# Last stage's pieces moved into the tile steps, with PSUM packed, on one core of Trainium2

## The chip, the cores and the metric

The kernel runs on one core of one Trainium2 chip. The metric is the device time of one execution in microseconds (us). Everything is FP32, apart from one projection whose operands are split into a high and a low FP32R part. Half a per cent, about 1.4 us, is near the limit of what can be measured.

## The reference

One block of a network over x of shape (8, 512, 128): a state-space mixer and then a small gated network, each with layer norms around it and a residual. Cut to what matters:

```
x  = x + layernorm(mixer(layernorm(x)))
x  = x + layernorm(ffn(layernorm(x)))

mixer: proj = x @ W_in ; z, x_raw, B, C, dt, lam, theta = split(proj)
       B, C normalised and rotated by cumulated angles; x_raw = silu(x_raw)
       y = within-chunk products (C.B masked by decay) @ x  +  C @ state of the chunks before
       y = rms(y * silu(z)) ;  out = y @ W_out
ffn:   xk, xr = mixes of x and of x one token earlier
       r = sigmoid(xr @ W_r) ; k = relu(xk @ W_k)^2 ; out = r * (k @ W_v)
```

## The kernel before

**Tiling.** A chunk is 64 tokens. A tile holds one chunk of two batches, 128 partitions in all. There are 8 chunks (`NC_`) and 4 pairs of batches (`NQ`), so 32 tiles (`NT`); tile n belongs to chunk n // 4, and a chunk of all eight batches is four tiles. The state of a pair runs from tile n to tile n + 4.

**Stages.** First, all of x is loaded, its statistics and transposes are made, and the tables of decays, step sizes and angles are computed for all tiles (to about 43 us). Second, the tiles, software-pipelined. Third, the last stage: the residual, the layer norm and the gated network for the eight chunks, also pipelined (`chunk(k, par)` on each engine, driven by `chunks`, line 292).

**The order of the tiles.** It is written out by hand. Each engine has a function `step`, and runs its steps in order; semaphores tie the engines together.

- TensorE, `step(n)`, line 970: `project_x(n+1)`, `turn(n+1)` (transposes of B and C), `project_bc(n+2)`, `y_turn(n-1)` (transposes of y), `mix(n)` (from the state, within the chunk, new state), `score(n+1)`, `y_out(n-1)` (output projection, line 967). `mix` of tile n waits for the state sum of the tiles before it (`p_added`, n), for the mask of its own tile and for both weighted products of x.
- VectorE, `step(n)`, line 1302: `state(n-1)` (sum of new and old state, line 1223), `summed_y(n-1)` (line 1231), `mask(n)` (line 1216), some pieces of the last stage when n is 28 or more, the first weighted product of x for n + 1 (line 1209), `biased(n+2)` (line 1192), the second product, `rotations(n+2)` (lines 1197 and 1202).
- ScalarE, `step(n)`, line 654: `late_o(n-2)` (evacuates the projection's output and sums its squares), `x_gate(n+1)` (SiLU of x, line 616), `turned(n+1)`, `copy_in(n+3)`, `late_yt(n-1)`, `state_part(n)`, `squares(n+2)` (line 605, waits for `biased`), `z_gate(n+2)`, `late_ysq(n-1)`.
- GpSimd, `step(n)`, line 441: `lower_part(n+3)`, `early(n+2)` (a power, line 400, waits for the squares), `gated(n)` (y, line 439, waits for `summed_y(n)`), `token_factors(n+2)` (weights of x, line 408), `decayed_z(n+2)`, `state(n)` (line 423), and behind that, for n from 28 to 30, `factors` (a power over the columns of two chunks, line 431).

So GpSimd's step n runs beside VectorE's step n + 1, as it needs the y summed there.

**The last stage** for a chunk: `factor_terms` (VectorE), `factors` (GpSimd, power), residual (VectorE with `residual` for chunks 0 and 1, GpSimd lines 488 and 492 for the others), `stats2` and `moments2` (VectorE), the power `rstd2` (GpSimd), `norm_bias` (VectorE), `normed` (ScalarE), transposes (TensorE, line 1007), `curT` and `prevT` (ScalarE copies; the first column of each batch in `prevT` by GpSimd's `carry`), k (lines 1022, 1025), r (lines 1028, 1030), ReLU and square (ScalarE), v (line 1013), tanh (ScalarE), gating and statistics (VectorE, lines 1400 and 1404), moments, a power (line 508), the last residual (line 1388), outputs (line 720) and two stores on SP. For chunk 0 the first steps are already written into tiles 28 to 32.

**PSUM.** Eight banks of 512 columns: 0 holds z, B and C, 1 holds x, 2 the turned B and C and the state part, 3 and 4 the scores, 5 the new state, 6 turned y and the output projection, 7 y. The last stage reuses 0 (transposes), 1 (k), 2 (r) and 3 (v) once the tiles are done.

`tiles(False)` is the branch that the inputs take; `tiles(True)` (`general`) is for larger decays.

Of the kernel before, what the change touches and what calls it, by code (L numbers as in the profile page):

```python
# [22 lines left out]
F32 = mybir.dt.float32  # L23
# [7 lines left out]
L = 64  # L31
# [19 lines left out]
FAC_POW = 3  # L51
# [34 lines left out]
def build(nc, x, w_in, a_log, dt_bias, bc_bias, w_out, w_r, w_k, w_v, mu, consts, out, force_general=False):  # L86
    ctx = ExitStack()
    with ctx:
# [68 lines left out]
        scores = ctx.enter_context(nc.psum_tensor("scores", [128, R, 512], F32))  # L157
        bank += [scores[:, r, :] for r in range(R)] + [ps(n) for n in range(5, 8)]
# [20 lines left out]
        TURN_BANKS, SCALAR_BANKS, W_BANKS = (0, 1, 4, 5), (2, 3, 7), (6, 0)  # L179
        s2 = sem("tables_scalar")  # L180
# [41 lines left out]
        def flat(buf):  # L222
# [51 lines left out]
        curT = sb("curT", 128, 2, B, L)  # L274
# [9 lines left out]
        cnames = ("scaled_o x1_first x1 stats mom pow norm_bias pow3 norm_bias3 normed tr_ps tr_sb carried shifted k_ps k_relu k_act r_ps th v_ps "  # L284
                  "f stats3 res outv").split()
# [6 lines left out]
        def chunks(eng, body):  # L292


            for k in range(2):
                body(k, k % 2)
            with eng.Fori(1, NC_ // 2 - 1) as cc:
                for par in range(2):
                    body(cc * 2 + par, par)
            for k in range(NC_ - 2, NC_ + 2):  # L300
                body(k, k % 2)

        def has(k, back=0):

            return not isinstance(k, int) or 0 <= k - back < NC_

        def norms(k):

            return slice(0 if has(k, -1) else NQ, 2 * NQ if has(k, 2) else NQ)
# [42 lines left out]
        def _(pool):  # L352
# [7 lines left out]
            nc.gpsimd.memset(curT[:, 1], 0.0).then_inc(S["st_zero"], 1)  # L360
# [67 lines left out]
            def factors(c):  # L428

                cols = slice(c * 2 * NQ, (c + 1) * 2 * NQ)  # L430
                nc.gpsimd.tensor_tensor(tokc[:, 7, cols], tokc[:, 6, cols], halfn[:, 0:2 * NQ],
                                        ALU.pow).then_inc(fac_p, 1)

# [7 lines left out]
            def step(n, q, general):  # L441
# [4 lines left out]
                if isinstance(n, int) and n == NT - 1:  # L446
                    pool.wait_ge(C["mom"], MOM)
                    rstd2(0)
# [7 lines left out]
                if isinstance(n, int) and 0 <= n - (NT - NQ) < NC_ // 2 - 1:  # L456
                    pool.wait_ge(fac_v, FAC_POW)
                    factors(n - (NT - NQ))

            def rstd2(k):  # L460

                wait_past(pool, C["normed"], k * NQ)
                nc.gpsimd.tensor_tensor(frs[:, 0:NQ], fmo[:, 5, 0:NQ], halfn[:, 0:NQ], ALU.pow).then_inc(C["pow"], 1)

            def tiles(general):
                for n in range(-2, NQ):
                    step(n, n % NQ, general)
                pool.wait_ge(S["weights"], 4)
                with pool.Fori(1, NC_ - 1) as c:
                    for q in range(NQ):  # L470
                        step(c * NQ + q, q, general)
                for n in range(NT - NQ, NT):
                    step(n, n % NQ, general)
# [10 lines left out]
            def residual(c):  # L484

                rows = bass.ds(c * NQ, NQ)
                pool.wait_ge(fac_p, c // 2 + 1 if isinstance(c, int) else NC_ // 2)
                nc.gpsimd.tensor_tensor(o_all[:, rows], o_all[:, rows],
                                        tokc[:, 7, rows].unsqueeze(2).broadcast_to([128, NQ, D]), ALU.mult)\
                    .then_inc(C["scaled_o"], 1)  # L490
                pool.wait_ge(C["scaled_o"], c - 1)
                nc.gpsimd.tensor_tensor(x_all[:, rows], o_all[:, rows], x_all[:, rows], ALU.add).then_inc(C["x1"], 1)

            def carry(k, par):

                wait_past(pool, C["r_ps"], k)
                nc.gpsimd.tensor_tensor(prevT[:, :, 0:1], curT[:, 1 - par, :, L - 1:L],
                                        one[:].unsqueeze(1).broadcast_to([128, B, 1]), ALU.mult).then_inc(C["carried"], 1)

            carry(0, 0)  # L500

            def chunk(k, par):
                if has(k, -2):
                    residual(k + 2)
                pool.wait_ge(C["mom"], (k + 2) * MOM)
                if has(k, 2):
                    wait_past(pool, C["res"], (k - 2) * NQ)
                    nc.gpsimd.tensor_tensor(frs[:, NQ:], fmo[:, 5, NQ:], halfn[:, 0:NQ], ALU.pow).then_inc(C["pow3"], 1)  # L508
                if has(k, -1):
                    rstd2(k + 1)  # L510
                if has(k) and not (isinstance(k, int) and k == 0):
                    carry(k, par)
                if isinstance(k, int) and k == 1:
                    pool.wait_ge(fac_v, 2 * FAC_POW)
                    factors(NC_ // 2 - 1)

            chunks(pool, chunk)

        @block.scalar
        def _(act):  # L520

            act.wait_ge(s_a, 16)
# [131 lines left out]
            def step(n, q):  # L654
# [8 lines left out]
                if within(n - 1):  # L663
                    late_yt(n - 1)
# [772 lines left out]
```

## Time and profile before

| what | value |
| --- | --- |
| median of 3 runs | 272.7 us (271.68 to 273.03) |
| profiled execution | 273.49 us |
| its span in the profile | 271.7 us |
| busy: TensorE, VectorE, ScalarE, GpSimd | 229.7, 196.6, 194.1, 168.1 us |
| mean granted clock of TensorE | 0.963 |
| tables until about | 43 us |
| first and last output projection of a tile | 57.0 and 207.25 us |

The profiled execution took 273.49 us and its records span 271.7 us, so 1.8 us lie around the span. Busy times of TensorE count every matmul from start to modelled end; they overlap, so a sum of durations is more than the time in which they ran, and the distance between starts is the better measure. A row of the timeline gives the start (us from the span's start), the time until the last of the group ended, the engine (PE is TensorE, PEld its weight loads, DVE is VectorE, ACT is ScalarE, POOL is GpSimd), the line, the operation, the tiles written and read, and in brackets how long the engine had been idle before and whose work ended that.

### The profile page before, as it was taken

The page shows a single profiled execution, that of the slowest core. Times are in us where ns is not written, and L with a number is a line of the kernel's source. Part 1 is how long each engine was busy: PE and PEld are TensorE (multiplying, and loading weights), DVE is VectorE, ACT ScalarE, POOL GpSimd, SP SyncE. Part 2 cuts the span into 40 slices and gives each one's busy share as a digit, 9 for nine tenths or more (in the row PEclk, how much of TensorE's full clock was granted, in tenths as well). Part 3 has the DMA queues.
Part 4 walks back from the last instruction along what each step waited for, and adds up shares of the span by engine and source line. Part 5 has one row for each costly group of instructions (what it writes and reads, how often), then busy time and mean ns, then how long its engine had stood idle before and what let it go on. Part 6 is the DMA issues. An engine that isn't in the chain of part 4 may idle for free.

```text
span 271.7 us, 7118 instructions
## 1 busy us (share of the span) xinstructions
PE 229.7 (85%) x1958; PEld 176.3 (65%) x1958; DVE 196.6 (72%) x593; ACT 194.1 (71%) x727; POOL 168.1 (62%) x281
## 2 busy tenths in 40 slices
PE   0995997789899999999999999999873798989930
PEld 0993343578678788787887878877652485657730
DVE  1699999967677676776767757679565758887761
ACT  2367387689787877878778788788554386979941
POOL 6423407586686867777687786877596476774120
PEclk9999599999999999999999999999999599999995
DMA  5960000000000000000000000000000000311122
GB/s 131 224 219 2 0 0 1 0 4 2 2 2 0 2 2 0 2 0 2 2 0 0 2 2 0 2 0 4 2 0 6 5 2 1 77 36 43 41 58 58
DMA packets 10159, 6.39 MB, mean 24 GB/s; under 512 B 832, under 2 KB 9824, under 8 KB 10128
## 3 DMA queue, kind: packets, MB, share of 16 engines
q1 hardware_dynamic: 9984, 5.77, 8.5%
q8 instruction: 18, 0.29, 0.5%
q0 software_dynamic: 144, 0.21, 0.4%
q14 instruction: 13, 0.11, 0.1%
HBM read 3.88 MB, written 2.10 MB: 22 GB/s over the span
## 4 chain that ended last, share of the span: by engine, by line
PE 45%; DVE 19%; issue 14%; ACT 10%; POOL 7%; DMA 2%; ACTq 1%; DVEq 1%; POOLq 1%
PE bank L886 10%; PE bank L790 6%; PE bank L967 6%; PE bank L874 6%; PE bank L880 5%; ACT bt L627 3%; DVE f L1388 3%; POOL frs L508 3%; ACT bank L616 2%; DVE ff L1400 2%; PE bank L757 2%; DVE fst L1404 2%; DMA w_sb<-w_in 2%; PE bank L749 1%; POOL rb L400 1%
## 5 line engine op out<-in xcount | busy, mean ns | idle before, releaser
L1209 DVE TENSOR_TENSOR x<-bank,wx 128x512 f32<-128x512 f32 x32 | 22.1, 690 | 35.5 <-ACT bank L616 31.3
L886 PE MATMUL bank<-x,sg 64*64 64x256 f32 x256 | 34.6, 385 | 0.0
L886 PE MATMUL bank<-xg,sg 64*64 64x256 f32 x256 | 33.9, 376 | 0.0
L874 PE MATMUL bank<-x,turned_bc 64*64 64x256 f32 x224 | 29.6, 376 | 0.0
L439 POOL TENSOR_TENSOR y<-ysum,zs 128x256 f32<-128x256 f32 x32 | 23.7, 740 | 7.7 <-DVE ysum L1231 7.2
L397 POOL TENSOR_TENSOR mse<-msb,eps_all 128x2 f32<-128x2 f32 x32 | 6.9, 217 | 33.1 <-ACT junk L607 33.1
L880 PE MATMUL bank<-st,bt 64*64 64x256 f32 x128 | 20.8, 395 | 5.0 <-ACT bt L627 4.9
L886 PEld LDWEIGHTS bank<-xg,sg 64*64 64x64 f32 x256 | 21.5, 133 | 4.7
L400 POOL TENSOR_TENSOR rb<-mse,halfn 128x2 f32<-128x2 f32 x32 | 23.0, 717 | 2.5
L616 ACT ACTIVATE bank<-bank,rsn 128x512 f32<-128x512 f32 x32 | 21.2, 661 | 4.3 <-PE bank L790 1.4
L967 PE MATMUL bank<-wo_sb,yt 128*128 128x128 f32 x128 | 22.8, 301 | 0.5 <-ACT yt L633 0.5
L1209 DVE TENSOR_TENSOR xg<-bank,wx 128x512 f32<-128x512 f32 x32 | 21.7, 680 | 0.0
L652 ACT ACTIVATE zt<-bank 128x256 f32<-128x256 f32 x32 | 12.3, 384 | 11.1 <-PE bank L880 11.1
L865 PE MATMUL scores<-bt 64*64 64x64 f32 x256 | 20.2, 230 | 0.0
L415 POOL TENSOR_TENSOR zs<-zs,ec_all 128x256 f32<-128x256 f32 x32 | 20.2, 631 | 0.0
L508 POOL TENSOR_TENSOR frs<-fmo,halfn 128x4 f32<-128x4 f32 x8 | 8.1, 1012 | 19.2 <-DVE fmo L325 19.2
L790 PE MATMUL bank<-w_hi,x_hi 128*128 128x512 f32 x32 | 15.3, 478 | 5.5 <-DVE w_lo L1093 2.7
L874 PEld LDWEIGHTS bank<-x,turned_bc 64*64 64x64 f32 x224 | 18.0, 133 | 1.4
L886 PEld LDWEIGHTS bank<-x,sg 64*64 64x64 f32 x256 | 17.9, 132 | 1.3
L967 PEld LDWEIGHTS bank<-wo_sb,yt 128*128 128x128 f32 x128 | 16.7, 190 | 3.1 <-ACT yt L633 0.7
L865 PEld LDWEIGHTS scores<-bt 64*64 64x64 f32 x256 | 16.7, 132 | 2.3 <-ACT bt L627 0.3
L423 POOL TENSOR_TENSOR st<-sp,f_all 128x256 f32<-128x256 f32 x28 | 17.6, 629 | 0.0
(201 smaller groups left out, 771.9 us busy)
## 6 DMA issues: line engine op xcount, KB each, us to landing
x_all<-x SPq DMA_DIRECT2D x16, 128.0 KB, 3.8
out<-o_all SPq DMA_DIRECT2D x16, 128.0 KB, 2.4
cm<-consts SPq DMA_DIRECT2D x1, 640.0 KB, 6.5
w_sb<-w_in SPq DMA_DIRECT2D x1, 480.0 KB, 4.4
cm<-consts POOLq DMA_DIRECT2D x1, 128.0 KB, 3.9
wo_sb<-w_out SPq DMA_DIRECT2D x1, 128.0 KB, 4.8
bcb_sb<-bc_bias SPq DMA_DIRECT2D x1, 96.0 KB, 4.7
wr_sb<-w_r SPq DMA_DIRECT2D x1, 64.0 KB, 4.6
```

The lines of the kernel that those rows point to most:

```text
L400: nc.gpsimd.tensor_tensor(rb[:, par], mse[:], halfn[:, 0:R], ALU.pow).then_inc(S["rb_ready"], 1)
L415: nc.gpsimd.tensor_tensor(zs[:, q].rearrange("p (h e) -> p h e", e=P), zs[:, q].rearrange("p (h e) -> p h e", e=P), at(ec_all, n).unsqueez ...
L423: nc.gpsimd.tensor_tensor(st[:, q].rearrange("p (h e) -> p h e", e=P), sp[:].rearrange("p (h e) -> p h e", e=P), at(f_all, i).unsqueeze(2) ...
L439: nc.gpsimd.tensor_tensor(y[:, par], ysum[:, par], zs[:, q], ALU.mult).then_inc(S["y_ready"], 1)
L616: nc.scalar.activation(bank[1][:], bank[1][:], ACT.Silu, scale=rsn[:, par:par + 1]).then_inc(S["x_silu"], 1)
L790: mm = nc.tensor.matmul(bank[1][:], a[:, par], b[:, O_X:O_S], start=(k == 0), stop=(k == 2))
L865: mm = nc.tensor.matmul(scores[half(h), r, 0:L], bt[half(r), par, r, half(h)], bt[half(r), par, 1 - r, half(h)], start=True, stop=True)
L874: mm = nc.tensor.matmul(bank[5][half(1 - h), 0:DI], turned_bc[half(h), q, 2 * r], rx(x, r)[half(h)], start=(r == 0), stop=(r == R - 1))
L880: mm = nc.tensor.matmul(to[half(h)], bt[half(1 - h), par, h, half(h)], state[half(1 - h)], start=True, stop=True)
L886: mm = nc.tensor.matmul(bank[7][half(h), 0:DI], sg[half(h), a, r], rx(x, r)[half(h)], start=start, stop=stop)
L967: mm = nc.tensor.matmul(bank[6][:, DI:DI + D], yt[:, k], wo_sb[:, k], start=(k == 0), stop=(k == 1))
L1209: vec.tensor_tensor((x1, xg)[a][:, par].rearrange("p (a e) -> p a e", e=P), bank[1][:].rearrange("p (a e) -> p a e", e=P), wx[:, par, a].u ...
```

## The change

The last stage is cut into pieces, one chunk at a time, and each piece is put into a step of the tiles, for all chunks. Each engine gets `ffn(n)`, with `c, q = divmod(n, 4)`; it goes on for 16 steps after the tiles (`FFN_STEPS`). The loops of VectorE, ScalarE and GpSimd over chunks are written out.

```
+FFN_STEPS = NT + 4 * NQ
 # TensorE, between project_bc(n + 2) and y_turn(n - 1)
+                ffn(n - 1)
+            def ffn(n):
+                c, q = divmod(n, NQ)
+                if q == 0 and valid(c - 3):
+                    project_v(c - 3)
+                if q == 1 and valid(c - 2):
+                    turn_normed(c - 2)
+                if q == 2 and valid(c - 2):
+                    project_k(c - 2)
+                if q == 3 and valid(c - 2):
+                    project_r(c - 2)
 # VectorE, between mask(n) and the first weighted product
+                ffn(n)
+            def ffn(n):
+                c, q = divmod(n, NQ)
+                if q == 0 and valid(c - 2):
+                    norm_bias(c - 2)
+                if q == 0 and valid(c - 4):
+                    last_residual(c - 4)
+                if q == 1 and valid(c - 3):
+                    gated_v(c - 3)
+                if q == 2 and valid(c - 1):
+                    factor_terms(c - 1)
+                if q == 2 and valid(c - 3):
+                    moments3(c - 3)
+                if q == 3 and valid(c - 1):
+                    residual(c - 1)
+                    stats2(c - 1)
+                    moments2(c - 1)
 # GpSimd, at the end of the step
+                ffn(n)
+            def ffn(n):
+                c, q = divmod(n, NQ)
+                if q == 1 and valid(c - 2):
+                    carry(c - 2)
+                if q == 2 and valid(c - 1):
+                    factors(c - 1)
+                if q == 2 and valid(c - 3):
+                    rstd3(c - 3)
+                if q == 3 and valid(c - 1):
+                    rstd2(c - 1)
 # ScalarE, between copy_in(n + 3) and late_yt(n - 1)
+            def empty_ffn_bank(n):
+                c, q = divmod(n, NQ)
+                if q == 0 and valid(c - 3):
+                    gate_r(c - 3)
+                if q == 2 and valid(c - 2):
+                    turned_x(c - 2)
+                if q == 3 and valid(c - 2):
+                    k_relu(c - 2)
 # ScalarE, at the end of the step
+            def ffn(n):
+                c, q = divmod(n, NQ)
+                if q == 0 and valid(c - 2):
+                    normed(c - 2)
+                if q == 1 and valid(c - 4):
+                    outputs(c - 4)
+                if q == 3 and valid(c - 2):
+                    k_square(c - 2)
```

The residual is done by VectorE for all chunks, and `factors` takes the four columns of one chunk:

```
             def factors(c):
+                pool.wait_ge(fac_v, FAC_STEPS * (c + 1))
+                nc.gpsimd.tensor_tensor(tokc[:, 7, tiles_in(c)], tokc[:, 6, tiles_in(c)], halfn[:, 0:NQ],
...
+            def residual(c):
+                dve.wait_ge(fac_p, c + 1)
...
+            def norm_bias(c):
+                dve.wait_ge(C["pow"], c + 1)
...
+            def gated_v(c):
+                dve.wait_ge(C["th"], c + 1)
+                dve.wait_ge(C["v_ps"], c + 1)
```

PSUM is packed so that one bank (7) is free for the pieces; only chunks 6 and 7 use separate banks for them. Turned y and the scores share banks 3 and 4, the new state and the output projection share bank 5, y moves to bank 6. The tables use other banks (`CUM_BANKS` and so on). With the packing come waits on TensorE:

```
+        yt_ps, scores = bank[3][:, 0:DI], pair[:, :, DI:DI + L]
+        p_ps, o_ps, fk_ps = bank[5][:, 0:DI], bank[5][:, DI:DI + D], bank[5][:, DI + D:DI + D + H]
+        y_ps, ffn_ps = bank[6][:, 0:DI], bank[7]
...
             def score(n, par):
+                wait_past(pe, S["yt_sb"], n - 1)
...
             def mix(n, q, par):
+                wait_past(pe, S["o_sb"], n - 1)
...
             def y_turn(i, par):
-                pe.wait_ge(S["o_sb"], i)
+                pe.wait_ge(S["sg_ready"], min(i + 2, NT))
...
-            def y_out(i):
+            def y_out(i, general):
                 pe.wait_ge(S["yt_sb"], i + 1)
+                    pe.wait_ge(S["p_added"], min(i + 2, NT - NQ))
+                pe.wait_ge(S["o_sb"], i)
```

## Rows read from the trace of the kernel before

**Rows 1.** The page's head: span of the profiled execution.

```profile
span 271.7 us, 7118 instructions
```

**Rows 2.** Busy time by stretch: stretch, length, busy time (instructions) by engine, PEclk, DMA share, GB/s.

```profile
core 0: us, PE busy (x) PEld busy (x) DVE busy (x) ACT busy (x) POOL busy (x), PEclk, DMA share, GB/s
100.00:150.00 50.00, 48.44 (x530) 39.88 (x528) 35.49 (x84) 40.32 (x189) 36.29 (x71) 1.00 0.01 2
```

**Rows 3.** Timeline of one tile, from one output projection to the next.

```profile
131.12 0.71 PE L967 MATMUL bank<-wo_sb,yt 128*128 128x128 f32 x4
...
132.62 0.66 ACT L616 ACTIVATE bank<-bank,rsn 128x512 f32<-128x512 f32 x1
...
133.19 0.38 PE L958 MATMUL bank<-cm,y 128*128 128x128 f32 x2
...
133.32 0.69 DVE L1209 TENSOR_TENSOR x<-bank,wx 128x512 f32<-128x512 f32 x1 [1.45 <-ACT bank L616]
133.40 0.63 POOL L423 TENSOR_TENSOR st<-sp,f_all 128x256 f32<-128x256 f32 x1
...
135.65 0.42 DVE L1223 TENSOR_TENSOR sp<-bank,st 128x256 f32<-128x256 f32 x1
...
135.95 0.71 PE L967 MATMUL bank<-wo_sb,yt 128*128 128x128 f32 x4
```

**Rows 4.** Timeline of TensorE from the last tile into the last stage.

```profile
207.25 0.71 PE L967 MATMUL bank<-wo_sb,yt 128*128 128x128 f32 x4 [0.47 <-ACT yt L633]
211.34 1.09 PE L1007 MATMUL bank<-cm,xn 128*128 128x128 f32 x4 [3.38 <-issue]
213.12 2.07 PE L1022 MATMUL bank<-curT,w_cur 128*128 128x512 f32 x2 [0.69 <-ACT curT L714]
```

**Rows 5.** Timeline of the last stage: VectorE's operations and GpSimd's power.

```profile
254.74 0.16 DVE L1384 SCALAR_TENSOR_TENSOR fnb<-fmo,frs 128x4 f32<-128x4 f32 x1 [1.12 <-POOL frs L508]
...
254.93 1.14 DVE L1388 SCALAR_TENSOR_TENSOR f<-ff,frs,x_all 128x128 f32<-128x128 f32 x4
...
256.21 0.88 DVE L1400 SCALAR_TENSOR_TENSOR ff<-th,scores 128x128 f32<-128x128 f32 x4
...
257.01 0.86 DVE L1404 BATCH_NORM_STATS2 fst<-ff 128x6 f32<-128x128 f32 x4
...
258.01 0.17 DVE L316 TENSOR_TENSOR fmo<-fst 128x4 f32<-128x4 f32 x1
...
258.93 1.01 POOL L508 TENSOR_TENSOR frs<-fmo,halfn 128x4 f32<-128x4 f32 x1 [4.05 <-DVE fmo L325]
```

**Rows 6.** Timeline of the last stage: TensorE's pieces.

```profile
254.15 0.60 PE L1007 MATMUL bank<-cm,xn 128*128 128x128 f32 x4
...
254.75 1.16 PE L1013 MATMUL scores<-wv_half,ka 128*128 128x128 f32 x8
...
255.74 1.09 PE L1022 MATMUL bank<-curT,w_cur 128*128 128x512 f32 x2
...
257.53 0.38 PE L1028 MATMUL bank<-w_cur,curT 128*128 128x128 f32 x2
...
259.31 1.06 PE L1013 MATMUL scores<-wv_half,ka 128*128 128x128 f32 x8
```

**Rows 7.** Timeline of tiles 28 and 29, where VectorE has the residual of chunk 0.

```profile
186.72 0.68 DVE L1209 TENSOR_TENSOR x<-bank,wx 128x512 f32<-128x512 f32 x1
...
191.57 1.64 POOL L431 TENSOR_TENSOR tokc<-tokc,halfn 128x8 f32<-128x8 f32 x1
...
193.24 1.14 DVE L1278 SCALAR_TENSOR_TENSOR x_all<-o_all,tokc,x_all 128x128 f32<-128x128 f32 x4 [3.06 <-POOL tokc L431]
194.30 0.68 DVE L1209 TENSOR_TENSOR x<-bank,wx 128x512 f32<-128x512 f32 x1
...
195.28 0.22 ACT L605 ACTIVATE junk<-bank 128x64 f32<-128x64 f32 x1 [2.17 <-DVE bc L1192]
```

**Rows 8.** Timeline of the last stage: a small VectorE operation beside a large one of GpSimd.

```profile
232.99 1.16 POOL L488 TENSOR_TENSOR o_all<-o_all,tokc  x1
233.15 1.02 DVE L1299 SCALAR_TENSOR_TENSOR fnb<-fmo,frs 128x4 f32<-128x4 f32 x1
```

More of the change, by code:

```diff
@@ L290, in build, with valid, tiles_in @@
         fac_v, fac_p = sem("factors_vector"), sem("factors_pool")
[L292 to L309, printed above, removed]
+        def valid(c):
+            return 0 <= c < NC_
+        def tiles_in(c):
+            return slice(c * NQ, c * NQ + NQ)
         def moments(dve, stats, mo, n, chain, base, eps):
@@ L455, in step @@
                     state(n, q)
[L456 to L463, printed above, removed]
-            def tiles(general):
[L466 to L472, printed above, removed]
+                ffn(n)
+            def tiles(general):
+                for n in range(-2, NT):
+                    if n == NQ:
+                        pool.wait_ge(S["weights"], 4)
                     step(n, n % NQ, general)
@@ L481, in _ @@
                 tiles(True)
[L484 to L517, printed above, removed]
+            for n in range(NT, FFN_STEPS):
+                ffn(n)
         @block.scalar
@@ L737, in _ @@
-            chunks(act, chunk)
         @block.tensor
@@ L789, in project_x @@
                 for k, (a, b) in enumerate(parts):
[L790 removed]
+                    mm = nc.tensor.matmul(x_ps[:], a[:, par], b[:, O_X:O_S], start=(k == 0), stop=(k == 2))
                 mm.then_inc(S["x_ps"], 1)
@@ L925, in token @@
                     wait_past(pe, G["st"], n)
-                    nc.tensor.matmul(bank[5][:, DI:DI + H], oh[:], s_all[:, i, 0:H], start=True, stop=True)\
+                    nc.tensor.matmul(fk_ps, oh[:], s_all[:, i, 0:H], start=True, stop=True)\
                         .then_inc(G["fk_ps"], 1)
@@ L966, in y_out, with turn_normed @@
                 for k in range(2):
-                    mm = nc.tensor.matmul(bank[6][:, DI:DI + D], yt[:, k], wo_sb[:, k], start=(k == 0), stop=(k == 1))
+                    mm = nc.tensor.matmul(o_ps, yt[:, k], wo_sb[:, k], start=(k == 0), stop=(k == 1))
                 mm.then_inc(S["o_ps"], 1)
+            cur = curT[:].rearrange("p b l -> p (b l)")
+            prev = prevT[:].rearrange("p b l -> p (b l)")
+            def turn_normed(c):
+                pe.wait_ge(C["normed"], c * NQ + NQ)
+                if c == 0:
+                    pe.wait_ge(S["weights"], 4)
+                else:
+                    pe.wait_ge(C["f"], c * NQ)
+                for q in range(NQ):
+                    mm = nc.tensor.transpose(ffn_bank("t", c)[:, q * 128:q * 128 + 128], xn2[:, q], c_("ident"))
+                mm.then_inc(C["tr_ps"], 1)
@@ new lines, in project_v @@
+            def project_v(c):
+                v_ps = ffn_bank("v", c)
+                pe.wait_ge(C["k_act"], c + 1)
+                if v_ps is ffn_ps:
+                    pe.wait_ge(C["th"], c + 1)
+                else:
+                    pe.wait_ge(C["f"], c * NQ)
+                for q in range(NQ):
+                    mm = nc.tensor.matmul(v_ps[:, q * D:q * D + D], ka[:, q * 128:q * 128 + 128], wv_half[:],
+                                          start=True, stop=True)
+                mm.then_inc(C["v_ps"], 1)
```

393 lines of the change are left out of this document (174 added, 219 removed).

## The prediction

> **What bounds the kernel now.** I read the page first (span 271.7 us [rows 1]), then busy time by stretch, then the timeline of one tile, of the last stage, and of the one place where the last stage already reaches into the tiles. In a stretch of tiles TensorE is busy 48.4 of 50 us [rows 2]: the reader should see that no other engine comes near that. A tile lasts 4.84 us, from one output projection (131.12) to the next (135.95) [rows 3]. The last projection stands at 207.25 and the span ends at 271.7 [rows 1, 4]: 64.4 us follow, for eight chunks.
>
> The second loop is nearly as long [rows 3]. Projection at 131.12, SiLU of x on ScalarE at 132.62, first product on VectorE at 133.32 after 1.45 idle, then products, bias and rotations, then the state sum (135.65 to 136.07). Today nobody on TensorE waits for that sum before the next tile's `mix`. This is the slack that matters.
>
> **What the change removes.** The 64.4 us behind the last projection. What stays there: the last tile's chunk needs its factors (0.4 us on VectorE, an estimate from three such small operations), a power (1.01), residual, statistics and moments (2.85: 1.14, 0.86 and 0.85, the last from 258.01 to shortly before the power at 258.93 [rows 5]), a second power, then four normalisations and, ahead of them in the queues, chunk 6. From the projection to the transposes of chunk 7 I take 11 us: 6.5 from those terms with the evacuation of o, the rest an estimate for ScalarE's four normalisations and chunk 6. From these transposes (254.15) to the end it is 17.5 us today [rows 1, 6] and stays so, since its chain is the same. With 1.5 for a slow clock, below, 30 us stay and 34.5 go.
>
> **What it adds to the tiles.** I call the steps of a group of four by their remainder.
>
> *TensorE.* Transposes 0.60, k 1.79, r 1.78, v 1.0 (differences of starts [rows 6]): 5.2 per chunk. A tile of 4.84 has some 0.16 idle in it (the 1.6 of 50 [rows 2] over ten tiles), so 4.68. Steps 1, 2, 3, 0 then need 5.7, 5.3, 6.5, 6.5 of it, 23.9 a group against 19.4.
>
> *Every step.* o now shares bank 5 with the state's sums, so `y_out(n-1)` waits for `p_added` of tile n, which VectorE writes at the end of its loop. The projection would start at 136.07 and a release (about 0.1, an estimate) instead of 135.95 [rows 3]: 5.07 per plain step, +0.23. More important: TensorE's slack towards VectorE is gone, and whatever holds VectorE in front of the product lengthens the step by as much as it exceeds 1.45. Behind the waiting projection stands the next tile's projection of x, so SiLU and VectorE start later too.
>
> *Step 3.* VectorE's `residual(c-1)` waits for `factors(c-1)`. GpSimd issues that at the end of its step 2, behind gate, weights, decayed z and state product. GpSimd's step n follows `summed_y(n)`, which VectorE does in step n+1. So VectorE arrives right after the mask, and the power still lies 3 us ahead. The trace has this very pattern once: product at 186.72, power of the factors from 191.57, VectorE idle 3.06, residual at 193.24, that is 6.52 after the product [rows 7]. There the power took 1.64 and no state product preceded it; here 0.63 and 1.01 make the same. Then 2.85 of work: 9.35 from product to product, +4.5. From group 2 on, ScalarE has the two copies of the turned x in the step before (about 1.1, an estimate from 512 columns as in the SiLU's 0.66), which holds its squares and so GpSimd's chain; that squares wait on VectorE's bias and hold GpSimd shows at 195.28 [rows 7]. I take +5.4.
>
> *Step 0.* `norm_bias(c-2)` waits for `rstd2`, again at the end of GpSimd's previous step: state product ends at 134.03, power until 135.04 (an estimate from both rows), where the product began at 133.32 [rows 3, 5]. 6.5 from product to release, 0.1 for itself, from group 4 on 1.25 for `last_residual`: 7.85, +3.0 (before group 4 +1.8).
>
> *Step 1.* `gated_v` waits for v of the same TensorE step, behind that tile's projections. v starts 2.07 after the output projection (131.12 to the turning of y at 133.19 [rows 3]) and ends 1.16 later [rows 6], then 0.80 and 0.86 of gating and statistics [rows 5]: product 4.95 after the projection, instead of 2.20. With 2.87 from product to projection: 7.8, +3.0, from group 3 on.
>
> *Step 2.* Small operations (1.2) fit into the 1.45. +0.25, and +0.65 from group 4, as four outputs sit ahead of ScalarE's SiLU.
>
> *Sum.* Group 0: +1.8, an estimate: `mixing_weights` and the last table wait stand before the sum that TensorE now waits for. Group 1: three plain steps and 4.5, +5.2. Group 2: 1.8, 0.25, 0.25, 5.4, +7.7. Group 3: 1.8, 3.0, 0.25, 5.4, +10.4. Groups 4 to 6: 3.0, 3.0, 0.65, 5.4, 12.05 each, 36.2. Group 7 to the last projection: 12.05 less 2.7, which is paid there already (186.72 to 194.30 is 7.6 for a 4.84 tile [rows 7]), and less 3, an estimate, since from tile 28 there is no new state sum to wait for and the projections end: +6.3. Together +67.6; with -34.5 it is +33.
>
> *The clock.* In step 3 TensorE has 6.5 of work in 10.2 us: about 4 us idle in one piece ahead of the projection. After 3.38 idle at 211.34 it ran at 1.2 instead of 2.4 GHz: four transposes took 1.09 for 0.60, a matmul of 512 columns in its two parts 2.07 for 1.09 [rows 4, 6]; with the next like it, and a start on r, I take 3 us lost. In step 0 it has 1.4 in hand, so a fall costs up to 1.6; there are five such places: 0 to 8, I take 4, as not each need fall.
>
> *At nothing.* Unrolled loops (TensorE's queue is unrolled today and is the fullest), the exchanged banks of the tables (`mix(0)` now waits for VectorE's whole turns, which stand before the first mask that it waits for anyway), the stores, which SP issues earlier with nothing behind them (cover: the tiles), and ScalarE's pieces, hidden by VectorE's waits; without that cover up to 1.6 in step 1.
>
> **The total.** 273.5 (the profiled execution, span 271.7) + 33 + 4 = 310.5; the median shown is 0.8 lower, so **309.5 us**. Bounds: clock 0 to 8, drain 27 to 36, step 3 at 9.35 or 11: 298 to 322.
>
> **A rule against the row.** The division into `residual` on VectorE frees GpSimd of two large operations, one of which held a small VectorE operation for 1.02 us [rows 8], where its kind takes 0.16 [rows 5]. But VectorE's residual now begins beside the power of `rstd3`. The row that shows a hold stands beside an operation of 512 columns, not beside a power of four, so my sum has none. The Trainium skill ("SBUF — State Buffer", Who interferes with whom) says that an operation of VectorE with two inputs in SBUF and a reading one of GpSimd exclude each other for their whole length. By that each residual waits the power out.
>
> **Rivals.** *Ports.* Every residual, seven in all, is held by up to 0.87 (1.02 less about 0.15 [rows 5, 8]): +6, 315. For: the 1.02. Against: powers of four columns move almost nothing.
>
> *The waits for GpSimd are covered* (the other side). If VectorE came to its pieces only after the powers, because the step before is long on TensorE, groups would go by TensorE alone: +4.5 for groups 3 to 6, +3 for the seventh, +6.4 for the first three: +27, less 34.5: 266. It decides from where the tiles grow by less than 34.5 in all, so the waits may cost 1 us per chunk beyond TensorE's own work, not my 7. For: step 3 needs 6.5 of TensorE anyway. Against: TensorE's pieces stand behind the projection of x, so they don't delay VectorE, and 3.06 idle was seen [rows 7].
>
> *Only the residual's wait costs.* Steps 0 and 1 go by TensorE (+1.6, +0.8), step 3 as above: about +50, less 34.5: 288. For: v and `norm_bias` have no row of their own kind. Against: both places follow from the written order.
>
> *It balances.* Between these, within 0.5%.
>
> **How the numbers follow.** My case 0.68, ports 0.10, residual alone 0.10, covered 0.09, balance 0.03. Half a per cent (1.4 us) is about what a measurement tells apart here. Faster 0.09, same 0.03, slower 0.88. Range: my case with its bounds, ports and residual alone, less tails: 286 to 326.
>
> **What would show it.** VectorE idle some 3 us before the residual and before `norm_bias`, released by GpSimd's powers, and some 2.4 us before `ff`, released by v; output projections released by the state sum; steps from group 4 on of about 7.9, 7.8, 5.5 and 10.2 us; TensorE under 80% busy from 110 us on; last projection near 279; some 30 us behind it. I am wrong if those waits are under 1 us, or groups last under 25 us.

## The result, and the profile after

The changed kernel takes 310.2 us (median of 4 runs, 308.53 to 311.03) against 272.6 us before (4 runs, 271.68 to 273.03): a ratio of 1.138, 95% interval 1.132 to 1.144. The prediction was 309.5 us, slower. The total is right, but the parts cancel: the tiles took 5.2 us less than predicted and what follows them 5.6 us more, as shown below.

The head of the page of the changed kernel, busy time by engine, where the span of before was 271.7 us [rows 1]:

```profile
span 309.2 us, 6645 instructions
PE 234.3 (76%) x1958; PEld 178.8 (58%) x1958; DVE 207.1 (67%) x665; ACT 193.2 (62%) x727; POOL 157.8 (51%) x273
```

No engine is busy for more than 76% of the span, so something waits. From the table of waits of the changed kernel (who waited, for whom: us in total, times, longest):

```profile
PE bank L961 <- issue: 36.0, 17, 4.5
DVE x_all L1300 <- POOL tokc L431: 21.1, 8, 3.9
DVE fnb L1318 <- POOL frs L439: 21.0, 8, 3.0
DVE ff L1326 <- PE bank L1008: 14.6, 4, 5.2
DVE ff L1326 <- issue: 10.2, 4, 2.6
```

VectorE waits 21 us for the power of the factors (L431), 21 us for that of the norm (L439) and 25 us for v (14.6 and 10.2). TensorE stands 36 us ahead of the output projection (L961), which the profile books under "issue": in the rows below the projection at 184.20 starts 0.09 us after the state sum (183.69 and 0.42 long) ends. Each of the three waits of VectorE is seen in the timeline of one group in the middle of the tiles (start, duration, engine, line, operation; in brackets the idle time before and who ended it). The rows are chosen: VectorE's waits, what ends them, and one projection.

```profile
177.51 1.01 POOL L431 TENSOR_TENSOR tokc<-tokc,halfn 128x4 f32<-128x4 f32 x1
178.49 1.01 POOL L446 TENSOR_TENSOR frs<-fmo,halfn 128x4 f32<-128x4 f32 x1
178.56 1.14 DVE L1300 SCALAR_TENSOR_TENSOR x_all<-o_all,tokc,x_all 128x128 f32<-128x128 f32 x4 [3.07 <-POOL tokc L431]
...
183.69 0.42 DVE L1243 TENSOR_TENSOR sp<-bank,st 128x256 f32<-128x256 f32 x1
184.20 0.68 PE L961 MATMUL bank<-wo_sb,yt 128*128 128x128 f32 x4 [3.13 <-issue]
186.74 1.01 POOL L439 TENSOR_TENSOR frs<-fmo,halfn 128x4 f32<-128x4 f32 x1
187.78 0.41 DVE L1318 SCALAR_TENSOR_TENSOR fnb<-fmo,frs 128x4 f32<-128x4 f32 x1 [3.01 <-POOL frs L439]
...
194.11 1.05 PE L1008 MATMUL bank<-wv_half,ka 128*128 128x128 f32 x8
195.27 0.88 DVE L1326 SCALAR_TENSOR_TENSOR ff<-th,bank 128x128 f32<-128x128 f32 x4 [2.57 <-issue]
```

The last wait is booked under "issue" too; it ends 0.11 us after v does (194.11 and 1.05 long). The output projections of this group start at 174.93, 184.20, 192.07, 199.68 and 205.63. Busy time in the first three of its steps (3, 0 and 1 by their remainder), in step 0 of group 3, and in the stretch behind the last projection (columns: start and end, length, then busy us and count of TensorE, its weight loads, VectorE, ScalarE and GpSimd, then the granted clock of TensorE, the DMA share and GB/s):

```profile
174.93:184.20 9.27, 6.14 (x54) 4.14 (x55) 5.96 (x23) 4.83 (x22) 6.06 (x10) 1.00 0.01 2
184.20:192.07 7.87, 7.80 (x67) 6.56 (x67) 4.83 (x15) 4.29 (x18) 4.06 (x9) 0.78 0.01 2
192.07:199.68 7.61, 5.61 (x58) 4.77 (x59) 5.00 (x17) 6.04 (x26) 4.29 (x8) 1.00 0.00 0
122.10:130.60 8.50, 8.48 (x66) 7.18 (x67) 3.53 (x10) 4.24 (x18) 4.04 (x9) 0.71 0.01 3
273.62:309.20 35.58, 17.61 (x76) 12.49 (x76) 14.61 (x78) 14.27 (x39) 5.49 (x7) 0.74 0.14 31
```

TensorE works 6.14 of 9.27 us in step 3 and 5.61 of 7.61 in step 1. In step 0 it is busy all the time, but its granted clock is 0.78: part of the step runs at 1.2 GHz, after the 3.13 us for which it stood ahead of 184.20. Step 0 of group 3 is the longest of its kind, 8.50 us at a granted clock of 0.71. A group lasts 30.7 us, where four tiles of before took 19.4. The last projection is at 273.62 (before: 207.25 [rows 4]), and 35.6 us follow it (before: 64.4).

### The profile page after: what moved, and what is told of

It is laid out like the page before. It is cut to its first block, busy times and chain, and to the rows that moved or that the text cites. A ratio compares the mean times of both kernels' runs of the same rounds, so it can differ in the third digit from the quotient of the medians.

```text
span 309.2 us, 6645 instructions
## 1 busy us (share of the span) xinstructions
PE 234.3 (76%) x1958; PEld 178.8 (58%) x1958; DVE 207.1 (67%) x665; ACT 193.2 (62%) x727; POOL 157.8 (51%) x273
## 4 chain that ended last, share of the span: by engine, by line
PE 52%; issue 22%; ACT 11%; DVE 10%; POOL 2%; DMA 1%; POOLq 0%; ACTq 0%; DVEq 0%
PE bank L874 7%; PE bank L961 6%; PE bank L779 6%; PE bank L862 5%; PE bank L868 5%; PE bank L771 4%; PE bank L994 3%; PE bank L996 2%; PE bank L985 2%; PE bank L986 2%; ACT xn L676 2%; PE bank L843 2%; ACT bank L605 2%; PE bank L746 2%; ACT bt L616 1%
## 5 line engine op out<-in xcount | busy, mean ns | idle before, releaser
L961 PE MATMUL bank<-wo_sb,yt 128*128 128x128 f32 x128 | 23.0, 304 | 37.6 <-issue 36.0
L397 POOL TENSOR_TENSOR mse<-msb,eps_all 128x2 f32<-128x2 f32 x32 | 8.6, 269 | 75.4 <-ACT junk L596 75.4
L961 PEld LDWEIGHTS bank<-wo_sb,yt 128*128 128x128 f32 x128 | 17.5, 198 | 41.4 <-issue 39.9
L874 PE MATMUL bank<-x,sg 64*64 64x256 f32 x256 | 35.2, 393 | 0.0
L594 ACT ACTIVATE junk<-bank 128x64 f32<-128x64 f32 x64 | 13.8, 226 | 25.5 <-DVE bc L1212 23.3
L605 ACT ACTIVATE bank<-bank,rsn 128x512 f32<-128x512 f32 x32 | 21.1, 659 | 7.7 <-PE bank L779 7.5
L400 POOL TENSOR_TENSOR rb<-mse,halfn 128x2 f32<-128x2 f32 x32 | 24.0, 749 | 2.5
L1326 DVE SCALAR_TENSOR_TENSOR ff<-th,bank 128x128 f32<-128x128 f32 x32 | 7.0, 282 | 24.8 <-PE bank L1008 14.6
L1300 DVE SCALAR_TENSOR_TENSOR x_all<-o_all,tokc,x_all 128x128 f32<-128x128 f32 x32 | 9.5, 359 | 21.1 <-POOL tokc L431 21.1
L874 PEld LDWEIGHTS bank<-xg,sg 64*64 64x64 f32 x256 | 19.9, 133 | 4.9
L862 PEld LDWEIGHTS bank<-x,turned_bc 64*64 64x64 f32 x224 | 17.0, 135 | 4.7 <-issue 0.5
L853 PE MATMUL pair<-bt 64*64 64x64 f32 x256 | 19.1, 230 | 0.0
L1217 DVE TENSOR_TENSOR rot<-bc,cs_all 128x384 f32<-128x384 f32 x32 | 17.6, 551 | 0.0
```

Of the source, the lines that this page charges most:

```text
L400: nc.gpsimd.tensor_tensor(rb[:, par], mse[:], halfn[:, 0:R], ALU.pow).then_inc(S["rb_ready"], 1)
L605: nc.scalar.activation(x_ps[:], x_ps[:], ACT.Silu, scale=rsn[:, par:par + 1]).then_inc(S["x_silu"], 1)
L853: mm = nc.tensor.matmul(scores[half(h), r], bt[half(r), par, r, half(h)], bt[half(r), par, 1 - r, half(h)], start=True, stop=True)
L862: mm = nc.tensor.matmul(p_ps[half(1 - h)], turned_bc[half(h), q, 2 * r], rx(x, r)[half(h)], start=(r == 0), stop=(r == R - 1))
L874: mm = nc.tensor.matmul(y_ps[half(h)], sg[half(h), a, r], rx(x, r)[half(h)], start=start, stop=stop)
L961: mm = nc.tensor.matmul(o_ps, yt[:, k], wo_sb[:, k], start=(k == 0), stop=(k == 1))
```

## The experiments

My theory after the result: the time goes to three waits for things that the written order delivers late (two powers at the end of GpSimd's previous step, v in the same step of TensorE), and to the wait of the output projection that couples TensorE to VectorE. The rivals: TensorE's work on the pieces, or VectorE held beside GpSimd. "Group" is steps 20 to 23 by the starts of the output projection, "last" the start of the last one, "behind" the span less that, all from the profiled execution. The ratios are against runs of before in the same set and on the same chip. The median of before itself moved by 0.8% between the sets (272.6 to 274.7 us), so a difference of one or two us between rows means little by itself.

| kernel | median us | ratio, 95% | group | last | behind |
|---|---|---|---|---|---|
| before | 272.6 | | 19.43 | 207.25 | 64.4 |
| b_wait | 282.1 | 1.027–1.037 | 20.54 | 216.34 | 65.6 |
| after | 310.2 | 1.132–1.144 | 30.70 | 273.62 | 35.6 |
| a_pool_early | 298.6 | 1.085–1.097 | 29.18 | 263.32 | 35.2 |
| a_pe_late | 296.9 | 1.078–1.090 | 28.22 | 264.52 | 31.7 |
| a_both | 281.2 | 1.022–1.032 | 26.05 | 249.00 | 30.5 |
| a_dve_end | 294.8 | 1.074–1.083 | 27.98 | 258.60 | 34.2 |
| a_shift | 279.1 | 1.014–1.024 | 25.18 | 243.10 | 34.8 |
| a_tail | 304.2 | 1.108–1.116 | 30.70 | 274.26 | 29.5 |
| a_defer | 304.4 | 1.108–1.121 | 29.73 | 268.76 | 33.8 |
| s_tail | 275.0 | 1.003–1.010 | 25.16 | 242.75 | 32.0 |
| s_tail_late | 275.5 | 1.005–1.012 | 25.51 | 242.51 | 30.1 |
| s_tail_defer | 272.1 | 0.994–1.000 | 24.94 | 238.27 | 31.7 |
| s_end_defer | 282.3 | 1.027–1.036 | 26.59 | 248.80 | 31.0 |

**The wait for the state sum alone, in the kernel before (b_wait).**

```
-            def y_out(i):
+            def y_out(i, general):
                 pe.wait_ge(S["yt_sb"], i + 1)
+                if not general:
+                    pe.wait_ge(S["p_added"], min(i + 2, NT - NQ))
```

> The kernel before, with one thing of the change: in the product branch the output projection waits for the state addition of the next tile (min(i + 2, 28) additions), its pieces staying in a last stage of their own. My theory takes this wait for the reason of the plain step of 5.0 us in the changed kernel against 4.84 before: about +0.17 us a tile in 28 tiles, so 277 us, range 274 to 281. Rival: the wait is free, because the addition has always come by then, and the 0.17 us comes from the packed PSUM banks: 272.6 us, unchanged.

282.1 us, above my range. The timeline of one tile of it:

```profile
152.26 0.42 DVE L1225 TENSOR_TENSOR sp<-bank,st 128x256 f32<-128x256 f32 x1 [0.20 <-issue]
152.83 0.68 PE L969 MATMUL bank<-wo_sb,yt 128*128 128x128 f32 x4 [0.48 <-DVE sp L1225]
```

The projection starts 0.15 us after the sum ends at 152.68; ahead of it TensorE stood 0.48. Tiles last 5.06, one in four 5.35: 5.8 us over steps 4 to 27. Another 2.6 us come in steps 2 and 3, which take 6.05 and 6.77 instead of 5.40 and 4.84 (group 0 of my sum has +1.8 there). The wait costs what I gave it and more. A plain step of the changed kernel takes 5.02 us, so the packed banks aren't needed to explain it. Why one tile in four takes 5.35 isn't shown.

**GpSimd's powers earlier (a_pool_early).**

```
                 if within(n + 2):
                     early(n + 2, q % 2)
+                ffn(n)
                 if within(n):
                     gated(n, q, q % 2)
...
-                ffn(n)
```

> The changed kernel; GpSimd issues the three powers and the carry of the last stage ahead of the product of its tile instead of at the end of its step. Computation unchanged. Theory (hand-order waits): VectorE no longer idles 3 us for the residual's factors and 3 us for the norm's factors in each group of four tiles; a steady group goes from 30.7 to some 26.5 us (its steps 9.3 to 7.0 and 7.9 to 6.0), the total to 289 us, range 284 to 297. Rival (the time is TensorE's own work on the pieces, or VectorE held beside the powers): no more than 3 us less than the changed kernel, 307 to 310.

298.6 us: faster, as theory and not rival has it, but 1.6 us above the upper end. The waits shrank: for the factors from 21.1 to 5.9 us, for the norm's power from 21.0 to 4.5. That is 31.7 us less of waiting for 11.6 us of time. The group didn't shrink to the 26.5 us expected: it alternates between 28.2 and 30.2 us. The page of this kernel shows where part of the rest went:

```profile
PE 231.6 (78%) x1958; PEld 175.3 (59%) x1958; DVE 221.4 (74%) x665; ACT 193.3 (65%) x727; POOL 158.5 (53%) x273
```

VectorE does the same work in 221.4 us that took it 207.1. In the timeline of one step 0:

```profile
178.01 0.73 POOL L474 TENSOR_TENSOR y<-ysum,zs 128x256 f32<-128x256 f32 x1
178.07 0.69 DVE L1318 SCALAR_TENSOR_TENSOR fnb<-fmo,frs 128x4 f32<-128x4 f32 x1 [0.57 <-POOL frs L439]
178.75 2.30 DVE L1344 SCALAR_TENSOR_TENSOR f<-ff,frs,x_all 128x128 f32<-128x128 f32 x4
179.06 0.68 POOL L415 TENSOR_TENSOR zs<-zs,ec_all 128x256 f32<-128x256 f32 x1
```

The four last residuals (L1344) take 2.30 us here and 1.13 in the changed kernel (188.18 there). They now stand beside GpSimd's products; in the changed kernel VectorE waited while these went by. So the wait had hidden a hold: an operation of VectorE that takes longer while one of GpSimd runs.

The same run shows what the clock costs in step 0. Here are two of its steps 0:

```profile
176.94:184.76 7.82, 7.80 (x67) 6.50 (x67) 6.34 (x15) 4.24 (x18) 4.14 (x9) 0.78 0.01 2
206.12:212.92 6.80, 6.20 (x67) 5.21 (x67) 6.20 (x15) 4.82 (x21) 4.72 (x9) 1.00 0.01 4
```

It is the same work, and VectorE waits 0.57 us for the norm's power in both: 7.82 us at a granted clock of 0.78, 6.80 at 1.00. TensorE's busy time is 1.6 us longer at the lower clock; 0.60 of that it had stood still ahead of the projection at 212.92, so the step is longer by 1.0.

**TensorE's pieces one place earlier (a_pe_late).**

```
-                ffn(n - 1)
                 if within(n - 1):
                     y_turn(n - 1, other)
...
                     score(n + 1, other)
+                ffn(n)
                 if within(n - 1):
                     y_out(n - 1, general)
```

> The changed kernel; TensorE issues a piece of the last stage behind the scores, ahead of the output projection of the same step, instead of in the next step behind the projections. Computation unchanged. Theory: v is there when VectorE asks for it, the step of 7.6 us falls to some 5.5 while the step with the turn may grow, so 1.5 to 2.5 us less in each of the last five groups and the V of chunk 5 lies ahead of the branch's end: total 298 us, range 294 to 303. Rival (the pieces' own TensorE time counts wherever they stand): 309 to 311.

296.9 us, in range. VectorE's wait for v falls from 24.8 to 9.9 us and the group from 30.7 to 28.2 us. V of chunk 5 now stands ahead of the branch's end, and 31.7 us follow the last projection instead of 35.6.

**Both (a_both).**

> The changed kernel with both earlier edits, GpSimd's powers ahead of its product and TensorE's pieces behind the scores of their own step. Computation unchanged. Each alone took some 12 to 13 us from the changed kernel. Theory: they act on different steps of a group (powers on steps 3 and 0, v on step 1), so they add: 285 us, range 281 to 290. Rival: they shorten the same wait of the ring, and a group is held by something else at 28 us: 292 to 297.

281.2 us, in range: 29.0 less than the changed kernel, where the single edits gave 11.6 and 13.3. They add, and 4 us more come. About 2 of these would be the clock: step 0 runs at a granted clock of 1.00 in each of the groups 4 to 7, where it was 0.78 in each of the changed kernel's and 0.78 and 0.79 in two of the four with the powers alone (7.82 and 7.68 us, where the other two take 6.8). Where the rest comes from isn't shown. The steps tie the engines into a ring with several waits in it, and shortening one leaves the next.

**VectorE's part at the end of its step (a_dve_end).** `ffn(n)` of VectorE moves from behind `mask(n)` to behind `rotations(n + 2)`.

> The changed kernel; VectorE issues its part of the last stage at the end of its step, behind the weighting of x and the rotations of the next tiles, instead of ahead of them. Computation unchanged. Theory: the factors, the norm's factors and v then come some 3 us before VectorE asks for them, at the price that the work lies ahead of the next tile's mask: a group of some 26 to 28 us instead of 30.7, total 290 us, range 280 to 296. Rival (VectorE's own work is in line wherever it stands, and the waits were only its slack): a group stays at 30 us or more, total 305 to 312.

294.8 us, in range, group 28.0. The waits fall more than with the powers earlier, to 1.9 us for the factors, 2.9 for the norm's power and 10.4 for v, but the pieces now lie ahead of the next tile's mask. I didn't take this price apart here; it comes back in the last run below.

**VectorE and ScalarE one tile later (a_shift).**

```
                 if within(n):
                     mask(n)
-                ffn(n)
+                ffn(n - 1)
...
 (ScalarE)       step(n, n % NQ)
-                ffn(n)
+                for m in ([n - 1] if n < NT else [n - 1, n] if n == NT else [n]):
+                    ffn(m)
```

> The changed kernel; VectorE and ScalarE issue their parts of the last stage (not the PSUM evacuations) one tile later inside the tiles, GpSimd and TensorE as they are. Computation unchanged. Theory: all three waits (both powers, v) get a tile of slack, the steady group is bound by TensorE's own work, some 24 to 25 us instead of 30.7, and the total is 275 us, range 269 to 283, with the 35 us behind the last projection as they were. Rival (VectorE's work in line with the tiles is the bound, waits or not): a group stays above 28 us, total over 295.

279.1 us, in range. The wait for the factors is nearly gone (0.4 us left), the one for the norm's power too (1.1), that for v is 6.5, and the last projection comes 30.5 us earlier. One step 0 of it, VectorE's residual of chunk c-1 beside GpSimd:

```profile
167.42 2.60 DVE L1301 SCALAR_TENSOR_TENSOR x_all<-o_all,tokc,x_all 128x128 f32<-128x128 f32 x4
167.46 0.74 POOL L474 TENSOR_TENSOR y<-ysum,zs 128x256 f32<-128x256 f32 x1
168.16 0.45 POOL L408 TENSOR_TENSOR wx<-w_all,rb 128x128 f32<-128x128 f32 x1
168.56 0.68 POOL L415 TENSOR_TENSOR zs<-zs,ec_all 128x256 f32<-128x256 f32 x1
169.20 0.68 POOL L423 TENSOR_TENSOR st<-sp,f_all 128x256 f32<-128x256 f32 x1
```

Four residuals take 2.60 us, next to four operations of GpSimd of 2.55 together. The residuals end at 168.34, 168.75, 169.38 and 170.02, each 0.14 us after an operation of GpSimd has ended. In the changed kernel the same four took 1.14 beside the power of `rstd3` (178.49 above). Over the kernel they average 0.626 us here, 0.359 there (rows of the groups by form, changed kernel first, then this one):

```profile
L1300 DVE SCALAR_TENSOR_TENSOR x_all<-o_all,tokc,x_all 128x128 f32<-128x128 f32 x32 | 9.5, 359 | 21.1 <-POOL tokc L431 21.1
```

```profile
L1301 DVE SCALAR_TENSOR_TENSOR x_all<-o_all,tokc,x_all 128x128 f32<-128x128 f32 x32 | 18.2, 626 | 0.4 <-POOL tokc L431 0.4
```

**The trailing steps inside the branches (a_tail).** On TensorE, GpSimd and VectorE:

```
             def tiles(general):
                 for n in range(-1, NT + 1):
                     step(n, general)
+                for n in range(NT, FFN_STEPS):
+                    ffn(n)
...
-            for n in range(NT, FFN_STEPS):
-                ffn(n)
```

> The changed kernel; the trailing steps of the last stage on TensorE, GpSimd and VectorE stand inside each of the two branches (product and general) instead of behind them. Computation and order unchanged. Theory: the 3 us in which TensorE does nothing behind the last tile come from leaving the branch, and V of chunk 5 and all behind it moves up by them: 307.2 us, range 306 to 308.5. Rival (another wait hides there): 310 us, unchanged.

304.2 us, twice the gain that I expected and below my range. TensorE behind the last projection, first in the changed kernel:

```profile
273.83 0.50 PE L961 MATMUL bank<-wo_sb,yt 128*128 128x128 f32 x3
277.34 2.05 PE L1008 MATMUL bank<-wv_half,ka 128*128 128x128 f32 x8 [3.01 <-issue]
280.52 1.08 PE L974 MATMUL bank<-cm,xn 128*128 128x128 f32 x4 [1.13 <-DVE ff L1326]
282.97 2.05 PE L985 MATMUL bank<-curT,w_cur 128*128 128x512 f32 x2 [1.36 <-ACT prevT L691]
...
291.10 0.66 PE L974 MATMUL bank<-cm,xn 128*128 128x128 f32 x4 [1.33 <-ACT xn L676]
```

and with the edit:

```profile
274.26 0.71 PE L959 MATMUL bank<-wo_sb,yt 128*128 128x128 f32 x4 [0.74 <-ACT yt L619]
274.81 1.06 PE L1006 MATMUL bank<-wv_half,ka 128*128 128x128 f32 x8
277.00 0.63 PE L972 MATMUL bank<-cm,xn 128*128 128x128 f32 x4 [1.13 <-DVE ff L1324]
278.99 1.10 PE L983 MATMUL bank<-curT,w_cur 128*128 128x512 f32 x2 [1.36 <-ACT prevT L689]
...
285.61 0.63 PE L972 MATMUL bank<-cm,xn 128*128 128x128 f32 x4 [1.99 <-DVE ff L1324]
```

The 3.01 us of standing still are gone, and the pieces behind them, V (v, L1008), T (the transposes, L974) and K (the first half of k, L985), take 1.06, 0.63 and 1.10 instead of 2.05, 1.08 and 2.05: they had run at 1.2 GHz (granted clock 0.50 from 277.34 to 285.00, 1.00 from 274.26 to 281.00 with the edit). From the last projection to the transposes of chunk 7 it is 17.5 us with the hole and 11.35 without, 6.1 less; 3.0 of it is the hole, and about as much is left for the lower clock. No input was late: the last that V waits for, the tanh of chunk 5, had ended at 273.30. The same hole stands in the kernel before, 3.38 us [rows 4], as "issue"; I had read it there and not asked what it was.

**The output projection one step later (a_defer).** `y_out(n - 2)` behind `project_x(n + 1)`, instead of `y_out(n - 1)` at the end of the step, and `y_out(NT - 1)` behind the loop.

> The changed kernel with the output projection one step later alone. Computation unchanged. Theory: of the changed kernel's 37 us only the part that the wait for the state addition costs comes back, 0.2 us in each step, mostly in those without a wait for a power or v: 306 us, range 303 to 309. Rival: this wait is what couples TensorE to the late VectorE, and most of the loss goes with it: under 295 us.

304.4 us, within 303 to 309: TensorE stands 3.7 us ahead of the projection instead of 36.0, and 5.8 us of time come back. So most of this wait only passes on what VectorE is late by.

**Towards a kernel that beats both.** s_tail has the edits of a_shift and a_tail; s_tail_late also has K and R behind the scores; s_tail_defer is s_tail with the edit of a_defer; s_end_defer is s_tail_defer with VectorE's part at the end of its step (a_dve_end's place).

> The same without that edit and with all four pieces of TensorE between the projection and the turning of y: the one-tile shift (279.1 us alone) with the trailing steps inside the branches, which took 6.0 us from the changed kernel (3 us of standing still and as much of TensorE at its lower clock behind it). Computation unchanged. Theory: the two edits touch different stretches and add: 273.5 us, range 271 to 276. Rival: the hole hides behind the shifted work of VectorE: 277 to 279.

> The changed kernel with VectorE's and ScalarE's parts of the last stage one tile later (279.1 us in the earlier run), the trailing steps inside the branches, and on TensorE the pieces K and R behind the scores of their own step (T and V stay between the projection and the turning of y). Computation unchanged. Theory: ScalarE no longer waits for K and R (11.6 and 10.5 us) ahead of copying the turned y, which gives 0.5 to 1 us a group, and the branch's end 3 us: 272 us, range 267 to 276, about level with the kernel before. Rival: VectorE, not ScalarE, holds the group at 25.2 us, and only the branch's 3 us come: 276 us.

> The changed kernel with VectorE's and ScalarE's parts of the last stage one tile later, the trailing steps inside the branches, and the output projection of a tile issued one step later, behind the next projection of x, where the state addition that it waits for is over. Computation unchanged. Theory: the kernel before with this wait alone lost 0.22 us a tile, because TensorE stood still between the scores and the output projection; with other work in that place the tiles without pieces fall from 5.0 to 4.8 us and those with pieces by up to as much, less where VectorE holds the group: 5 us less than the same kernel without the edit, 270 us, range 266 to 273, which is faster than the kernel before. Rival: VectorE holds the steps with its own work, and nothing is gained in them: 274 to 276 us.

> The kernel of 272.1 us (ScalarE's part one tile later, trailing steps in the branches, output projection one step later) with VectorE's part at the end of its step, behind the weighting and the rotations, instead of ahead of them in the next step: some 3 us earlier, and away from the three large products of GpSimd. Computation unchanged. Theory: the four residuals, of 0.71 us each in the median where they stand beside those products and 0.34 us where they stand behind them, give back some 1.3 us in each of seven groups, of which VectorE's line passes on most: 265 us, range 260 to 270. Rival: ahead of the next mask the same work costs TensorE as much as it saves, as in the run with this edit alone, whose groups stayed at 28 us: 272 to 285 us.

s_tail: 275.0, in range, 4.1 less than a_shift. s_tail_late: 275.5, nothing gained, as its rival has it: the group is 25.5. s_tail_defer: 272.1, in range. I had expected it to be faster than the kernel before; with a ratio of 0.997 (0.994 to 1.000) it is level and not clearly faster. s_end_defer: 282.3, a miss of 17 us on my theory, and within its rival's 272 to 285. The residuals took 1.13 us a group again,

```profile
166.27 1.13 DVE L1300 SCALAR_TENSOR_TENSOR x_all<-o_all,tokc,x_all 128x128 f32<-128x128 f32 x4
...
169.74 0.41 DVE L1236 TENSOR_TENSOR sg<-pair,cm 128x256 f32<-128x256 f32 x1
171.43 0.69 DVE L1229 TENSOR_TENSOR x<-bank,wx 128x512 f32<-128x512 f32 x1 [1.28 <-ACT bank L603]
```

but in this place all of VectorE's part lies ahead of the state sum, y's sum and the mask. The mask comes at 169.74, 3.47 us after the residual's start, and what follows in the ring comes as much later: VectorE then idles 1.28 us for ScalarE's SiLU. The step with the residual is 8.4 us where s_tail_defer has 6.98. What the hold costs and what its removal would give without this price stays open; no order with both was tried.

## Why the prediction was right

*The waits.* Predicted: VectorE idle some 3 us ahead of the residual and of `norm_bias`, some 2.4 ahead of `ff`. Measured 3.07, 3.01 and 2.57. a_both and a_shift show that they are the cause and not a symptom: with them short or gone, at the same work, the time falls by 29 to 31 us.

*The steps* from group 4 on, predicted 7.9, 7.8, 5.5 and 10.2, measured 7.87, 7.61, 5.95 and 9.27: 30.7 against 31.4 a group. Two terms were off. In step 3 I had added 0.9 because ScalarE's copies of the turned x would hold GpSimd's chain. That came once, in group 2, where step 3 took 10.26 us and GpSimd began its product for y 0.92 us after VectorE's sum of y (112.07 to 112.99). From group 3 on the distance is 0.13 (175.16 to 175.29) and step 3 takes 9.3, since VectorE is itself later in step 2. There "small operations (1.2) fit into the 1.45" failed: with the moments of the last norm among them they took 2.64 us, from 200.16 to 202.80, and the product of x followed without a gap. Step 2 grew from 5.01 us in group 2 to 5.95. Several of the small operations were held by GpSimd's products, as here:

```profile
201.05 0.63 POOL L415 TENSOR_TENSOR zs<-zs,ec_all 128x256 f32<-128x256 f32 x1
201.11 0.60 DVE L317 TENSOR_TENSOR fmo<-fst 128x4 f32<-128x4 f32 x1
...
202.80 0.68 DVE L1229 TENSOR_TENSOR x<-bank,wx 128x512 f32<-128x512 f32 x1
```

The operation at 201.11 takes 0.60 us, where it takes 0.16 with GpSimd idle (168.40 in s_end_defer). The groups 0 to 3 came out at +2.2, +4.4, +8.8 and +12.0 (predicted 1.8, 5.2, 7.7, 10.4), 4 to 6 at +33.8 in all (36.2), the last one at +5.3 (6.3).

*The clock.* I added 4 us for it. It did fall in step 0, to a mean of 0.78 in each of the groups 4 to 7, but there TensorE's slower work ends together with VectorE's late state sum (191.97, projection at 192.07): both fill 7.87 us, and nothing is added. The step of the prediction that failed is "in step 0 it has 1.4 in hand, so a fall costs up to 1.6": the two windows of a_pool_early give 1.6 for the fall, and the 1.4 in hand had to be taken off it. In groups 2 and 3 VectorE has no last residual in step 0 and comes sooner, so there the clock did cost time. Step 0 took 7.12 and 8.50 us where my sum has 6.6, and in it VectorE waited 0.54 and 1.92 us for TensorE's new state, the second time here:

```profile
130.08 0.42 DVE L1243 TENSOR_TENSOR sp<-bank,st 128x256 f32<-128x256 f32 x1 [1.92 <-PE bank L862]
```

That is up to 2.5 us, paid in two groups, and it is why these groups came out above the sum.

*The last projection* was predicted near 279 and came at 273.6, 5.2 us sooner. The clock's 4 us were added on top of the tiles' 67.6, and the tiles took 66.4 with the clock in it. Less the clock's 2.5 that is some 64: the waits were put 3 to 4 us too high, most of it in groups 4 to 7, and the clock 1.5.

*Behind it* I predicted 30 us and 35.6 came. From the transposes of chunk 7 to the end it is 18.1 (291.10 to 309.2), as good as the 17.5 of the prediction. The failed step is "from the projection to the transposes of chunk 7 I take 11 us", with 1.5 for a slow clock besides: it took 17.5. V of chunk 5 and its gating stand there first, behind the end of the branch. a_tail, without the hole, has 11.35 (274.26 to 285.61).

So +5.6 and -5.2 cancelled, and the 0.7 us between forecast and median is luck. (310.5 less 0.8 is also 309.7, and not the 309.5 that I wrote.) The sign is not luck: it rests on the waits.

*The shares.* The last projections of before, b_wait, a_shift and the changed kernel are at 207.25, 216.34, 243.10 and 273.62. By these steps the wait for the state sum costs 9.1 us, the three late deliveries 30.5, and 26.8 lie between: the pieces' own work in the ring, the packed banks and the holds beside GpSimd, which no run takes apart. The shares depend on the order of the steps: in the changed kernel a_defer gets 5.8 us back, not 9.1. Against them stand 28.8 us less behind the projection (64.4 to 35.6). Even with the late deliveries all but gone the other two, 35.9, outweigh these: a_shift is slower than before, and only with the branch's end and the deferred projection is it level.

*The rivals.* "The waits are covered" (266) is refuted by the waits. "Only the residual's wait costs" (288) is refuted by step 1, which lasted 7.61 us with TensorE standing 1.82 ahead of the projection. Step 0's 7.87 alone wouldn't do, since TensorE at the lower clock fills it; there the evidence is the 3.01 us of waiting for the norm's power. "Ports", as I put it, is refuted in the changed kernel: no residual took over 0.55 us, and two took 0.61 together while the power ran. It was right that VectorE can be held by GpSimd, and wrong about the partner, as the last section shows.

## What to carry to other kernels

When work is woven into a ring of engines, write down for each new wait when its producer issues in its own order, not how long it takes: a power of 1 us cost VectorE 3 us of waiting here, twice in four tiles, because it was written behind its engine's other work. Give such consumers a whole step of slack before weaving anything in; it was worth 31 us. Count a fall of the clock only by what is left of it once the waits of the same step are taken off.

## What was unexpected of the hardware

*A hold depends on the partner.* Beside GpSimd's products of 128 to 256 columns four residuals with two tensors in SBUF took 2.60 us, beside a power of four columns 1.14. The Trainium skill ("SBUF — State Buffer", Who interferes with whom) says that a VectorE operation with two inputs in SBUF contends with one of GpSimd that reads SBUF, under an exclusive lock. The products agree: one residual per operation of GpSimd, 2.60 against 2.55. The power of 1.01 us (178.49 in the changed kernel) doesn't: two residuals ran in 0.61 us beside it, 178.56 to 179.17. Why the power doesn't hold them isn't shown. A wait can hide such a hold: VectorE's busy time grew by 14.3 us when the powers came early.

*Behind the end of the branch TensorE stands still for about 3 us.* It is 3.38 us in the kernel before, 3.01 in the changed one and 2.87 to 3.10 in b_wait, a_shift, a_dve_end and a_defer, and it goes when nothing stands behind the branch (a_tail). The Trainium skill ("Runtime: NRT & Kernel Launch", Instruction fetch mechanics) says that a taken branch with a target outside what is already fetched makes the engine wait for a fetch. That fits, since the other branch's code lies between; no run shows the fetch itself.

*The clock follows the hole.* After 3 us of standing, V, T and the first half of K took nearly twice their time (2.05, 1.08 and 2.05 for 1.06, 0.63 and 1.10), so the hole cost 6 us, not 3.
